# Scan states in SBUF, the C row in a PSUM bank, products with C on pairs of tiles

## The chip, the cores and the metric

One core of one Trainium2 chip runs the whole program. The metric is the device time of one execution in microseconds. The engines of the core work side by side and meet at semaphores: TensorE (PE) multiplies matrices, VectorE (DVE), ScalarE (ACT) and GpSimd (POOL) work on tiles, SyncE (SP) issues most DMAs.

## The reference

The input is x of 8 sequences of 512 positions and 512 features. Three parts are added to it one after the other:

```python
x = x + 0.5 * ffn(layernorm(x))          # G
x = x + attn(layernorm(x))               # M: a state-space layer
x = x + 0.5 * ffn(layernorm(x))          # F

# ffn: h = silu(x @ w_gate) * (x @ w_up); of each 4 neighbours the 2 of largest magnitude stay; h @ w_down
# attn:
skip = xn @ W_skip.T;  u = silu(causal_conv4(xn @ W_in.T) + conv_b)
delta = softplus(u @ Wd1.T @ Wd2.T + bd2);  Bt = u @ WB.T;  Ct = u @ WC.T;  A = -exp(A_log)
h[l] = exp(delta[l] * A) * h[l-1] + (delta[l] * u[l]) * B[l]     # 1024 channels x 16 states
y[l] = sum over the 16 states of h[l] * C[l]
out = ((y + u * W_D) * silu(skip)) @ W_out.T
```

All of it is fp32.

## The kernel before

Features lie on the 128 partitions and the 512 positions of a sequence on the free axis, so a tile is 128x512 f32 and fills one PSUM bank. The sequences b = 0 to 7 pass through three stages: G (first FFN), M (the state-space layer) and F (second FFN). `ORDER` lists the 16 FFNs. The program is a list of 575 ticks that class `Plan` writes out by hand-set numbers; every engine's block walks the same ticks and issues, in its own fixed order, what the tick holds. A tick holds one product (a gate or up tile of an FFN, 12 matmuls, L678 `product`), side jobs (`win`, `down`, `in`, `skip`, `dt`, `bc`, `dl`, `out` and the norms' sums), and some units of the scan. `PAUSES` puts ticks without a product between, `STARTS[b]` is the tick at which the scans of sequence b begin, and `VECTOR`, `TENSOR` and `READ` are the planner's costs: by them it deals the units out to the ticks and chooses side banks.

A **unit** is one scan of a 128x512 tile: one of 8 channel tiles with one of 16 states, so 128 units a sequence and 1024 in all, in two halves of 64 a sequence. Four neighbouring units (HE) share a state and thus one row of B and of C; `load_rows` (ACT's DMA queue) brings both rows, broadcast over the partitions, to `scan_rows`. A unit u goes through four engines:

- ScalarE, `unit` (L911): `decay[u % 3]`, a PSUM bank, gets exp(delta * A). It waits until the product with C of unit u - 3 has read the bank (L920). `upto` issues these up to two units ahead of the scans (EXP_LEAD).
- GpSimd, `scan_input` (L1450): `scan_in[u % 4]` = du * B, once scan u - 4 is done.
- VectorE, `scan` (L1330): the scan, in place in the PSUM bank `decay`.
- VectorE, `times_c` (L1336): `scan_out[u % 6]` = state * C row, 128x512, once GpSimd has freed that slot (L1342).
- GpSimd, `sum_states` (L1462): adds two slots at once to `y`, 128x1024. It is issued three pairs late (LAG).

VectorE's queue holds, in each tick, the units in four shares (`begin`, `finish`), and between them: `select` (L1276), `add_down` (L1311), `add_out` (L1320), `centre`, `compare` (L1264), `input_low` and `x_low` (zlo, xlo: what the rounded high parts leave), `multiply` (L1257), `gate`, `delta_times_u` and the taps of the convolution (L1359). In `begin` a share of two units runs scan, scan, product, product; a share of one unit runs scan, other work if the tick has any, product.

FFN products and projections are made of three matmuls for each of the 4 k: high weights with the high part of the input, high weights with its low part (`zlo`, `xlo`), low weights with the high part (L690 to L692, L795 to L797). The first product of an FFN waits for `zlo` tile by tile (L689). The wins of the 2-of-4 selection (L743) wait for all three comparisons, the first `down` of a stage (L772) for all four selections.

The convolution's output goes to `cv[e % 2]` and from there to DRAM (L553), `skip` through `skb` (L545, L1087). PSUM has eight banks: five for products and side jobs, three for `decay`.

Of the kernel before, what the change touches and what calls it, by code (L numbers as in the profile page):

```python
# [19 lines left out]
B, L, D = 8, 512, 512  # L20
E, N, DT, DC = 1024, 16, 128, 4
I = 2048
P = 128
KD = D // P
# [12 lines left out]
BANKS = 3  # L37
# [27 lines left out]
PAUSES = {0: 9, 34: 1, 45: 7, 224: 4, 384: 1, 416: 1, 448: 4, 480: 24}  # L65
# [13 lines left out]
STARTS = (67, 130, 191, 250, 312, 359, 409, 454, 515)  # L79
# [7 lines left out]
VECTOR = {"mean": 2.3, "down": 0.3, "out": 0.7, "win": 0.6, "in": 1.1, "up": 0.7, "step": 2.9, "low": 2.0, "scale": 3.0, "gate": 2.2, "du": 3.0, "unit": 1.99}  # L87
TENSOR = {"dt": 6.9, "bc": 1.8, "fold": 1.2, "msum": 0.9, "mean": 0.6, "vsum": 0.9, "var": 0.9, "dl": 0.0, "win": 0.7, "down": 3.5, "in": 3.5, "skip": 3.5,
          "out": 3.5, "product": 2.8}
READ = {"win": 0.2, "down": 0.25, "out": 0.25, "mean": 0.3, "msum": 0.1, "vsum": 0.1, "in": 0.9, "var": 1.9, "skip": 0.6, "dt": 0.6, "bc": 0.6, "fold": 0.6, "dl": 0.6,  # L90
        "gate": 0.35, "up": 1.35, "first up": 0.55}
# [212 lines left out]
def build(nc, x_in, ffn_w, down_w, mam_w, out_w, wdt_in, wbc_in, wd2_in, small_in, out):  # L304
# [6 lines left out]
    with ctx:  # L311
# [6 lines left out]
        def pb(name):  # L318
# [61 lines left out]
        decay = [pb(f"decay{k}") for k in range(BANKS)]  # L380

# [5 lines left out]
            "decay_ready", "input_ready", "state_ready", "weighted_ready", "sum_ready",  # L387
# [6 lines left out]
            "skip_stored", "u_stored_0", "u_stored_1", "u_loaded_0", "u_loaded_1", "u_loaded_2",  # L394
# [28 lines left out]
        def conv_of(b, e):  # L423

            return cv[e % 2][:] if b else du[:, e, :]
# [41 lines left out]
        def u_stores(b, e):  # L467

            return 4 * (b - 1) + e // 2 if b else 0
# [8 lines left out]
        def _(sp):  # L478
# [60 lines left out]
            for tick in range(plan.ticks):  # L539
                n = plan.product_at[tick]  # L540
                jobs = plan.jobs_at[tick - 1] if tick else []
                for key in plan.jobs_at[tick - 2] if tick > 1 else []:
                    if key[0] == "skip":
                        wait_read(sp, key)
                        sp.dma_start(skip_dram[key[1]][:, key[2], :], skb[:]).then_inc(sem["skip_stored"], 16)  # L545
# [3 lines left out]
                for key in plan.jobs_at[tick - 5] if tick > 4 else []:  # L549
                    if key[0] == "in" and key[1]:  # L550
                        b, e = key[1:]
                        sp.wait_ge(sem["u_ready"], KE * b + e + 1)
                        sp.dma_start(u_dram[b % 2][:, e, :], cv[e % 2][:]).then_inc(sem[f"u_stored_{e % 2}"], 16)  # L553
# [79 lines left out]
                for b in range(B):  # L633
# [12 lines left out]
                    if b + 1 < B and tick == max(plan.out_at[b, 0] + KD, plan.tick_of_job["in", b + 1, KE - 1] + 6):  # L646
                        for k in range(2):
                            sp.wait_ge(sem[f"u_stored_{k}"], 16 * 4 * (b + 1))
# [910 lines left out]
```

## Time and profile before

| | us |
|---|---|
| median of 3 runs | 3488.46 (3487.1 to 3489.23) |
| the profiled execution | 3488.33 |
| its span, first to last instruction | 3486.3 |
| granted TensorE clock, mean over the span | 0.988 |

| engine | busy us | share |
|---|---|---|
| TensorE | 3331.9 | 96% |
| VectorE | 2999.3 | 86% |
| GpSimd | 2584.7 | 74% |
| ScalarE | 1992.0 | 57% |

The times of single instructions are those of the profile. An instruction's duration runs to the acknowledgement of its writes, and the next one on the same engine may start before that, so durations of neighbours overlap; how far is seen from the starts in the timeline. A wait's releaser is the instruction whose semaphore came last.

### The profile page before, as it was taken

What the parts mean: (1) busy time and instruction counts of PE and PEld (TensorE: products, weight loads), DVE (VectorE), ACT (ScalarE), POOL (GpSimd) and SP (SyncE); (2) the same over time, 40 slices, a digit from 0 to 9 for tenths busy, and PEclk for the clock granted to TensorE, in tenths of its full rate; (3) what the DMA queues carried; (4) which work ended last, traced back from release to release, by engine and by line L of the source; (5) the groups of instructions that cost most, each with busy time, mean ns of one, the idle gap of its engine ahead of it and who ended that gap; (6) DMA issues with size and microseconds to landing.
All of it is one profiled execution on the core that took longest, in us unless ns stands there. A gap on an engine that the chain in (4) does not pass through costs nothing. (4 is left out here: it accounts for less than half of the span.)

```text
span 3486.3 us, 38913 instructions
## 1 busy us (share of the span) xinstructions
PE 3331.9 (96%) x11958; PEld 2112.4 (61%) x12020; DVE 2999.3 (86%) x3549; ACT 1992.0 (57%) x2755; POOL 2584.7 (74%) x1625
## 2 busy tenths in 40 slices
PE   8999999999999999999999998999989889989899
PEld 6775656557656665566656665556555555555467
DVE  4646998789889899989989999999999998999934
ACT  5545657557565574666555675566465575554422
POOL 1315786667887778778787898888889888989913
PEclk9999999999999999999999999999999999999999
DMA  9655566646756566467566675656646566655433
GB/s 362 223 194 190 167 218 212 230 170 219 234 179 230 177 228 233 151 221 224 199 212 204 198 242 178 212 172 222 225 140 220 175 215 212 181 159 191 135 122 117
DMA packets 243469, 696.44 MB, mean 200 GB/s; under 512 B 23536, under 2 KB 23792, under 8 KB 233584
## 3 DMA queue, kind: packets, MB, share of 16 engines
q1 hardware_dynamic: 173632, 559.72, 46.2%
q10 hardware_dynamic: 69632, 134.23, 14.4%
q8 instruction: 99, 1.62, 0.2%
q14 instruction: 106, 0.87, 0.1%
HBM read 619.94 MB, written 76.55 MB: 200 GB/s over the span
## 5 line engine op out<-in xcount | busy, mean ns | idle before, releaser
L1460 POOL TENSOR_TENSOR scan_in<-du,scan_rows 128x512 f32<-128x512 f32 x1024 | 1309.6, 1295 | 602.3 <-DVE decay L1333 506.5
L1333 DVE TENSOR_TENSOR_SCAN decay<-decay,scan_in 128x512 f32<-128x512 f32 x1024 | 1246.0, 1221 | 16.9 <-POOL scan_in L1460 8.7
L1473 POOL TENSOR_TENSOR y<-y,scan_out 128x1024 f32<-128x1024 f32 x512 | 1223.8, 2390 | 0.9 <-DVE scan_out L1343 0.9
L921 ACT ACTIVATE decay<-delta,small 128x512 f32<-128x512 f32 x1024 | 696.9, 688 | 866.8 <-DVE scan_out L1343 859.4
L690 PE MATMUL side<-zhi,wunit 128*128 128x512 f32 x2048 | 906.3, 443 | 36.5 <-DVE zlo L1237 12.8
L780 PE MATMUL side<-h,wdown 128*128 128x512 f32 x1760 | 800.4, 598 | 22.5 <-DVE res_r L1318 11.2
L692 PE MATMUL side<-zhi,wunit 128*128 128x512 f32 x2048 | 816.4, 399 | 0.0
L691 PE MATMUL side<-zlo,wunit 128*128 128x512 f32 x2048 | 815.3, 398 | 0.0
L1343 DVE TENSOR_TENSOR scan_out<-decay,scan_rows 128x512 f32<-128x512 f32 x1024 | 700.6, 685 | 36.3 <-POOL y L1473 14.2
L780 PEld LDWEIGHTS side<-h,wdown 128*128 128x128 f32 x1760 | 333.2, 191 | 392.5 <-issue 348.5
L908 ACT ACT_TABLE_LOAD x402 | 515.8, 1283 | 7.1
L690 PEld LDWEIGHTS side<-zhi,wunit 128*128 128x128 f32 x2048 | 388.8, 190 | 203.6 <-issue 81.6
L691 PEld LDWEIGHTS side<-zlo,wunit 128*128 128x128 f32 x2048 | 389.6, 190 | 126.4 <-issue 42.6
L692 PEld LDWEIGHTS side<-zhi,wunit 128*128 128x128 f32 x2048 | 389.1, 190 | 94.9
L1273 DVE TENSOR_TENSOR cmp<-ab,side 128x512 bf16<-128x512 f32 (+2 forms) x192 | 232.4, 1210 | 41.6 <-ACT side L968 41.4
L795 PE MATMUL side<-xhi,wmam 128*128 128x512 f32 x512 | 235.8, 461 | 18.4 <-DVE cv L1367 6.0
L808 PE MATMUL side<-y,wmam 128*128 128x512 f32 x512 | 232.9, 599 | 13.2 <-DVE y L1375 6.4
L1478 POOL TENSOR_TENSOR hlo<-h,hhi 128x512 fp32r<-128x512 f32 x32 | 45.3, 1442 | 253.3 <-ACT hhi L1020 253.2
L968 ACT ACTIVATE side<-h 128x512 f32<-128x512 f32 x192 | 113.1, 589 | 179.3 <-DVE h L1261 179.0
L751 PE MATMUL side<-cmp,signs 128*128 128x512 bf16 x670 | 173.8, 395 | 37.2 <-DVE cmp L1273 19.5
L797 PE MATMUL side<-xhi,wmam 128*128 128x512 f32 x512 | 204.8, 400 | 0.0
L796 PE MATMUL side<-xlo,wmam 128*128 128x512 f32 x512 | 203.9, 398 | 0.0
(109 smaller groups left out, 2828.3 us busy)
## 6 DMA issues: line engine op xcount, KB each, us to landing
wunit<-hl_dram SPq DMA_DIRECT2D x480, 512.0 KB, 4.1
scan_rows<-bc_dram ACTq DMA_DIRECT2D x256, 512.0 KB, 5.6
wdown<-down_w_dram SPq DMA_DIRECT2D x256, 256.0 KB, 3.0
wmam<-mam_dram SPq DMA_DIRECT2D x128, 512.0 KB, 4.2
hl_dram<-wunit SPq DMA_DIRECT2D x32, 512.0 KB, 5.9
skip_dram<-skb SPq DMA_DIRECT2D x64, 256.0 KB, 4.3
delta<-skip_dram SPq DMA_DIRECT2D x16, 1024.0 KB, 8.0
wmam<-wout_dram SPq DMA_DIRECT2D x32, 512.0 KB, 4.4
```

What stands on the lines that cost most here:

```text
L690: nc.tensor.matmul(main(n)[:], hi[:, k, :], zhi[:, k, :], start=(k == 0), stop=False)
L691: nc.tensor.matmul(main(n)[:], hi[:, k, :], zlo[:, k, :], start=False, stop=False)
L692: mm = nc.tensor.matmul(main(n)[:], lo[:, k, :], zhi[:, k, :], start=False, stop=(k == KD - 1))
L780: mm = nc.tensor.matmul(bank[:], wdown[t][:, j, :], h[s % 2][:, j, :], start=(j == 0), stop=(j == 3))
L795: nc.tensor.matmul(bank[:], w[:, k, :], xhi[:, k, :], start=(k == 0), stop=False)
L808: mm = nc.tensor.matmul(bank[:], w[:, odd * KD + t, :].bitcast(f32), y[:, e, :], start=(c + odd == 0), stop=(c + odd == 2))
L908: nc.scalar.preload_act_table_set(name)
L921: nc.scalar.activation(decay[u % BANKS][:], delta[:, e, :], ACT.Exp, scale=aneg[:, e * N + n:e * N + n + 1]).then_inc(sem["decay_ready"], 1)
L1333: nc.vector.tensor_tensor_scan(decay[u % BANKS][:], decay[u % BANKS][:], db[u % INPUTS][:], 0.0, ALU.mult, ALU.add).then_inc(sem["state_re ...
L1343: nc.vector.tensor_tensor(pr[u % RING][:], decay[u % BANKS][:], rows[m % ROWS][:, 1, :], ALU.mult).then_inc(sem["weighted_ready"], 1)
L1460: nc.gpsimd.tensor_tensor(db[u % INPUTS][:], du[:, e, :], rows[m % ROWS][:, 0, :], ALU.mult).then_inc(sem["input_ready"], 1)
L1473: nc.gpsimd.tensor_tensor(y[:, e:e + 2, :], y[:, e:e + 2, :], scan_out[:, k:k + 2, :], ALU.add).then_inc(sem["sum_ready"], 1)
```

## The change

- The scan writes its states to `scan_out[u % 6]` in SBUF and no longer over `decay`. So the even scan of a pair waits for the slot pair (`sum_ready`), and a `decay` bank is free after the scan. There are two `decay` banks instead of three.
- The freed bank, `decay_row`, holds the C row. ScalarE copies it from `scan_rows` once for four units (`copy_c_row`), after the last product with the row before, and ahead of the exponentials of the share.
- The product with C is made in place in `scan_out`, 128x1024, with the row broadcast over two tiles: 512 instead of 1024 instructions. Inside a share it comes after the next even scan, else at the share's end.
- A third buffer `cv` for the convolution takes the place of `skb`; `skip` rows pass through `zm` (first sequence) or `dts` (others), with waits for that.
- TensorE's order in products and projections: all high parts first, the matmuls with the low part of the input last; the first product of an FFN waits for the high parts, then for the low ones. The wins and the first `down` wait for their inputs one by one.
- Planner numbers: three pauses, three starts by one tick, costs and read times.

```diff
-BANKS = 3
+TAPS = 3
+BANKS = 2
+C_AFTER = 0
-PAUSES = {0: 9, 34: 1, 45: 7, 224: 4, 384: 1, 416: 1, 448: 4, 480: 24}
+PAUSES = {0: 9, 36: 1, 45: 7, 224: 4, 392: 1, 416: 1, 452: 4, 480: 24}
-STARTS = (67, 130, 191, 250, 312, 359, 409, 454, 515)
+STARTS = (67, 130, 191, 250, 311, 359, 408, 454, 516)
-VECTOR = {"mean": 2.3, "down": 0.3, "out": 0.7, "win": 0.6, "in": 1.1, "up": 0.7, "step": 2.9, "low": 2.0, "scale": 3.0, "gate": 2.2, "du": 3.0, "unit": 1.99}
+VECTOR = {"mean": 2.0, "down": 0.3, "out": 0.7, "win": 0.5, "in": 0.0, "up": 0.0, "step": 3.2, "low": 2.0, "scale": 3.3, "gate": 2.9, "du": 2.0,
+          "unit": 1.99}
...
-        cv = [sb(f"cv{k}", [P, L]) for k in range(2)]
-        skb = sb("skb", [P, L])
+        cv = [sb(f"cv{k}", [P, L]) for k in range(TAPS)]
+        skip_buffer = lambda b: dts[:] if b else zm[:, 0, :]
+        c_row = pb("decay_row")
...
                 for k in range(KD):
                     if n % FFN == 0:
+                        pe.wait_ge(sem["high_part_ready"], KD * i + k + 1)
+                    nc.tensor.matmul(main(n)[:], hi[:, k, :], zhi[:, k, :], start=(k == 0), stop=False)
+                    nc.tensor.matmul(main(n)[:], lo[:, k, :], zhi[:, k, :], start=False, stop=False)
+                for k in range(KD):
+                    if n % FFN == 0:
                         pe.wait_ge(sem["normed_ready"], KD * i + k + 1)
-                    nc.tensor.matmul(main(n)[:], hi[:, k, :], zhi[:, k, :], start=(k == 0), stop=False)
-                    nc.tensor.matmul(main(n)[:], hi[:, k, :], zlo[:, k, :], start=False, stop=False)
-                    mm = nc.tensor.matmul(main(n)[:], lo[:, k, :], zhi[:, k, :], start=False, stop=(k == KD - 1))
+                    mm = nc.tensor.matmul(main(n)[:], hi[:, k, :], zlo[:, k, :], start=False, stop=(k == KD - 1))
                 mm.then_inc(sem["product_ready"], 1)
...
-                if j == 0:
-                    pe.wait_ge(sem["compared"], 3 * s + 3)
+                    if j == 0:
+                        pe.wait_ge(sem["compared"], 3 * s + k + 1)
...
-                    act.wait_ge(sem["weighted_ready"], u - BANKS + 1)
+                    act.wait_ge(sem["state_ready"], u - BANKS + 1)
...
+            def copy_c_row(m):
+
+                act.wait_ge(sem[f"rows_loaded_{m % ROWS}"], 16 * (m // ROWS + 1))
+                if m:
+                    act.wait_ge(sem["weighted_ready"], HE * m)
+                nc.scalar.activation(c_row[:], rows[m % ROWS][:, 1, :], ACT.Copy).then_inc(sem["c_row_ready"], 1)
...
             def upto(end):
 
+                while HE * copied[0] + C_AFTER < end:
+                    copy_c_row(copied[0])
+                    copied[0] += 1
...
-                    act.wait_ge(sem[f"u_stored_{e % 2}"], 16 * u_stores(b, e))
+                    act.wait_ge(sem[f"u_stored_{e % TAPS}"], 16 * u_stores(b, e))
...
-                nc.scalar.activation(skb[:], bank_of(key)[:], ACT.Silu).then_inc(read_of(key), 1)
+                if e == 0:
+                    if b:
+                        wait_job(act, ("dl", b - 1, KE - 1))
+                    else:
+                        act.wait_ge(sem["x_low_ready"], KD)
+                nc.scalar.activation(skip_buffer(b), bank_of(key)[:], ACT.Silu).then_inc(read_of(key), 1)
...
+                if key[1]:
+                    act.wait_ge(sem["skip_stored"], 16 * KE * (key[1] + 1))
                 nc.scalar.activation(dts[:], bank_of(key)[:], ACT.Copy).then_inc(read_of(key), 1)
...
             def scan(u):
                 dve.wait_ge(sem["decay_ready"], u + 1)
                 dve.wait_ge(sem["input_ready"], u + 1)
-                nc.vector.tensor_tensor_scan(decay[u % BANKS][:], decay[u % BANKS][:], db[u % INPUTS][:], 0.0, ALU.mult,
+                if u >= RING and u % 2 == 0:
+                    dve.wait_ge(sem["sum_ready"], (u - RING) // 2 + 1)
+                nc.vector.tensor_tensor_scan(pr[u % RING][:], decay[u % BANKS][:], db[u % INPUTS][:], 0.0, ALU.mult,
                                              ALU.add).then_inc(sem["state_ready"], 1)
 
-            def times_c(u):
-                m = u // HE
-                if u % HE == 0:
-                    dve.wait_ge(sem[f"rows_loaded_{m % ROWS}"], 16 * (m // ROWS + 1))
-                dve.wait_ge(sem["state_ready"], u + 1)
-                if u >= RING:
-                    dve.wait_ge(sem["sum_ready"], (u - RING) // 2 + 1)
-                nc.vector.tensor_tensor(pr[u % RING][:], decay[u % BANKS][:], rows[m % ROWS][:, 1, :], ALU.mult).then_inc(sem["weighted_ready"], 1)
+            def times_c(p):
+                u = 2 * p
+                k = u % RING
+                dve.wait_ge(sem["c_row_ready"], u // HE + 1)
+                dve.wait_ge(sem["state_ready"], u + 2)
+                nc.vector.tensor_tensor(scan_out[:, k:k + 2, :], scan_out[:, k:k + 2, :], c_row[:].unsqueeze(1).broadcast_to([P, 2, L]),
+                                        ALU.mult).then_inc(sem["weighted_ready"], 2)
 
             def begin(units):
 
                 for u in units:
-                    second = (u - units.start) % 2
-                    if u > units.start and not second:
-                        times_c(u - 1)
                     scan(u)
-                    if second:
-                        times_c(u - 1)
+                    if u % 2 == 0 and u > units.start:
+                        times_c(u // 2 - 1)
 
             def finish(units):
-                if units:
-                    times_c(units[-1])
+                if units and units[-1] % 2:
+                    times_c(units[-1] // 2)
```

## Rows read from the trace of the kernel before

**Rows 1.** The page's first part: busy us, share of the span, instructions.

```profile
PE 3331.9 (96%) x11958; PEld 2112.4 (61%) x12020; DVE 2999.3 (86%) x3549; ACT 1992.0 (57%) x2755; POOL 2584.7 (74%) x1625
```

**Rows 2.** By stretch: length, busy us (count) of each engine, clock, DMA share, GB/s.

```profile
300.00:2080.00 1780.00, 1751.48 (x6298) 1103.05 (x6331) 1618.53 (x1910) 1097.11 (x1480) 1402.94 (x867) 1.00 0.63 207
...
2080.00:3280.00 1200.00, 1106.97 (x3777) 673.57 (x3797) 1142.73 (x1324) 694.55 (x953) 1057.74 (x655) 0.97 0.60 193
3280.00:3486.00 206.00, 186.94 (x708) 128.89 (x708) 96.00 (x136) 56.73 (x96) 64.17 (x44) 0.98 0.34 110
```

**Rows 3.** Timeline of VectorE: start us, us, line, operation, out<-in, how many merged.

```profile
2612.56 1.22 DVE L1333 TENSOR_TENSOR_SCAN decay<-decay,scan_in 128x512 f32<-128x512 f32 x1
2613.82 0.69 DVE L1343 TENSOR_TENSOR scan_out<-decay,scan_rows 128x512 f32<-128x512 f32 x1
2614.42 1.22 DVE L1333 TENSOR_TENSOR_SCAN decay<-decay,scan_in 128x512 f32<-128x512 f32 x1
...
2916.28 2.34 DVE L1333 TENSOR_TENSOR_SCAN decay<-decay,scan_in 128x512 f32<-128x512 f32 x2
```

**Rows 4.** Groups by line and form: busy us, mean ns | idle before, releasers.

```profile
L1333 DVE TENSOR_TENSOR_SCAN decay<-decay,scan_in 128x512 f32<-128x512 f32 x1024 | 1246.0, 1221 | 16.9 <-POOL scan_in L1460 8.7 <-ACT decay L921 8.0
...
L1343 DVE TENSOR_TENSOR scan_out<-decay,scan_rows 128x512 f32<-128x512 f32 x1024 | 700.6, 685 | 36.3 <-POOL y L1473 14.2
...
L908 ACT ACT_TABLE_LOAD x402 | 515.8, 1283 | 7.1
...
L968 ACT ACTIVATE side<-h 128x512 f32<-128x512 f32 x192 | 113.1, 589 | 179.3 <-DVE h L1261 179.0
...
L1273 DVE TENSOR_TENSOR cmp<-ab,side 128x1024 bf16<-128x1024 f32 x64 | 77.4, 1210 | 12.8 <-ACT side L968 12.8
...
L1231 DVE TENSOR_TENSOR zm<-zm,side 128x2048 f32<-128x2048 f32 x14 | 31.9, 2278 | 0.0
...
L1228 DVE TENSOR_TENSOR zm<-zm,side 128x512 f32<-128x512 f32 x8 | 5.0, 682 | 11.0 <-ACT side L1062 11.0
...
L1309 DVE TENSOR_TENSOR hlo<-h,hhi 128x512 fp32r<-128x512 f32 x4 | 2.7, 688 | 0.3 <-ACT hhi L1020 0.3
```

**Rows 5.** Waits between 2080 and 3280 us: who waited for whom, us, times, longest.

```profile
DVE scan_out L1343 <- POOL y L1473: 10.9, 13, 1.7
```

**Rows 6.** Timelines of VectorE and GpSimd: scans against the sums that free their slots.

```profile
2923.14 1.22 DVE L1333 TENSOR_TENSOR_SCAN decay<-decay,scan_in 128x512 f32<-128x512 f32 x1
2924.27 0.67 DVE L1318 SCALAR_TENSOR_TENSOR res_r<-side,res_r 128x512 f32<-128x512 f32 x1
2926.68 0.69 DVE L1343 TENSOR_TENSOR scan_out<-decay,scan_rows 128x512 f32<-128x512 f32 x1 [1.73 <-POOL y L1473]
...
2924.20 2.38 POOL L1473 TENSOR_TENSOR y<-y,scan_out 128x1024 f32<-128x1024 f32 x1
...
1918.90 1.22 DVE L1333 TENSOR_TENSOR_SCAN decay<-decay,scan_in 128x512 f32<-128x512 f32 x1
...
1916.64 2.37 POOL L1473 TENSOR_TENSOR y<-y,scan_out 128x1024 f32<-128x1024 f32 x1
...
3283.53 1.22 DVE L1333 TENSOR_TENSOR_SCAN decay<-decay,scan_in 128x512 f32<-128x512 f32 x1
...
3282.56 2.34 POOL L1473 TENSOR_TENSOR y<-y,scan_out 128x1024 f32<-128x1024 f32 x1
```

**Rows 7.** Waits over the whole span, longest in total first.

```profile
ACT decay L921 <- DVE scan_out L1343: 859.4, 544, 6.3
...
ACT cv L1073 <- DMA u_dram<-cv: 15.6, 8, 3.8
...
PE side L690 <- DVE zlo L1237: 12.8, 5, 6.7
...
DVE decay L1333 <- ACT decay L921: 8.0, 8, 1.9
...
PE side L795 <- DVE cv L1367: 6.0, 2, 3.9
```

More of the change, by code:

```diff
@@ L85 @@
 SPLIT_AT = 10
-VECTOR = {"mean": 2.3, "down": 0.3, "out": 0.7, "win": 0.6, "in": 1.1, "up": 0.7, "step": 2.9, "low": 2.0, "scale": 3.0, "gate": 2.2, "du": 3.0, "unit": 1.99}
[L88 to L91, printed above, removed]
+VECTOR = {"mean": 2.0, "down": 0.3, "out": 0.7, "win": 0.5, "in": 0.0, "up": 0.0, "step": 3.2, "low": 2.0, "scale": 3.3, "gate": 2.9, "du": 2.0,
+          "unit": 1.99}
+TENSOR = {"dt": 7.6, "bc": 1.2, "fold": 1.2, "msum": 0.9, "mean": 0.6, "vsum": 0.9, "var": 0.9, "dl": 0.0, "win": 0.7, "down": 3.5, "in": 3.2,
+          "skip": 3.6, "out": 3.9, "product": 2.8}
+READ = {"win": 0.1, "down": 0.2, "out": 0.25, "mean": 0.9, "msum": 0.2, "vsum": 0.5, "in": 0.9, "var": 1.9, "skip": 0.5, "dt": 0.3, "bc": 0.8,
+          "fold": 0.3, "dl": 0.6, "gate": 0.15, "up": 1.35, "first up": 0.75}
 EXP_TABLE, SILU_TABLE, SOFTPLUS_TABLE = "natural_log_exp_and_others", "silu_and_others", "softplus"
@@ L423, in conv_of @@
         def conv_of(b, e):
[L425 removed]
+            return cv[e % TAPS][:] if b else du[:, e, :]
         def last_down(i):
@@ L646, in _ @@
                     if b + 1 < B and tick == max(plan.out_at[b, 0] + KD, plan.tick_of_job["in", b + 1, KE - 1] + 6):
-                        for k in range(2):
-                            sp.wait_ge(sem[f"u_stored_{k}"], 16 * 4 * (b + 1))
+                        for k in range(TAPS):
+                            sp.wait_ge(sem[f"u_stored_{k}"], 16 * len(range(k, KE, TAPS)) * (b + 1))
                         sp.wait_ge(sem["input_ready"], UNITS * b + HALF)
@@ L793, in project @@
                     if kind == "in" and e == 0:
+                        pe.wait_ge(sem["x_high_ready"], KD * b + k + 1)
+                    nc.tensor.matmul(bank[:], w[:, k, :], xhi[:, k, :], start=(k == 0), stop=False)
+                    nc.tensor.matmul(bank[:], w[:, KD + k, :], xhi[:, k, :], start=False, stop=False)
+                for k in range(KD):
+                    if kind == "in" and e == 0:
                         pe.wait_ge(sem["x_low_ready"], KD * b + k + 1)
-                    nc.tensor.matmul(bank[:], w[:, k, :], xhi[:, k, :], start=(k == 0), stop=False)
-                    nc.tensor.matmul(bank[:], w[:, k, :], xlo[:, k, :], start=False, stop=False)
-                    mm = nc.tensor.matmul(bank[:], w[:, KD + k, :], xhi[:, k, :], start=False, stop=(k == KD - 1))
+                    mm = nc.tensor.matmul(bank[:], w[:, k, :], xlo[:, k, :], start=False, stop=(k == KD - 1))
                 mm.then_inc(sem["side_ready"], 1)
```

24 lines of the change are left out of this document (13 added, 11 removed).

## The prediction, made before the changed kernel ran

> **What bounds the kernel now.** I read the page's first part first. TensorE is busy 96% of the span, VectorE 86%, GpSimd 74%, ScalarE 57%: no engine has much to give, and the shares are means over stages [rows 1]. So next the busy time by stretches [rows 2]. From 300 to 2080 us TensorE is busy 1751 of 1780 us at a full clock; VectorE, at 1619, has 161 us to spare. That stretch is TensorE's, and a cheaper VectorE buys there at most the 28 us in which TensorE stands. From 2080 to 3280 us it is the other way round: VectorE is busy 1143 of 1200 us (57 idle), TensorE 1107 at a granted clock of 0.97 (93 idle), GpSimd 1058. Each sequence of 128 scans has fewer products beside it there, so VectorE sets the pace and TensorE waits for its results. The last 206 us hold the tail, with few scans. The change must therefore be costed on VectorE's queue between 2080 and 3280 us. GpSimd ran 655 instructions there, two inputs and one sum for each pair of units, so some 437 units or 218 pairs.
>
> Third, what a VectorE instruction costs. The listed durations overlap: three neighbours in [rows 3] start 1.26 us (scan, then its own product with C) and 0.60 us (product, then next scan) apart, and two merged scans take 2.34 us, so 2.34 - 1.22 = 1.12 us is one scan's real share and 0.60 that of a product with C. A scan that is directly followed by a product that needs its own result costs 1.26 and not 1.12: the product waits out the scan's end, 0.13 us more. Over the run 477 of the 1024 scans are followed so (counted in the timeline; [rows 3] shows one).
>
> **The change part by part.**
>
> *Products with C, 1024 of 128x512 become 512 of 128x1024.* The nearest forms are the 128x1024 comparison, 1210 ns, and the scaling of `zm`, 682 ns for 128x512 and 2278 ns for 128x2048 (an SBUF tensor in place, with a PSUM operand broadcast over it: the new form), which gives 1.04 ns an element and 1214 ns for 1024 [rows 4]. The duration falls by 2 x 685 - 1214 = 156 ns a pair, and a reader of busy shares would book 80 us for the run. But 0.09 us of each duration is overlap with the next instruction, so the queue gains 2 x 0.595 - 1.125 = 0.065 us a pair: 218 x 0.065 = 14 us in the VectorE stretch, 33 in the run. Bounds: 12 to 34 (all the duration).
>
> *Fewer direct waits.* At most one product a pair can now stand right behind its own scan. At the old share of 477/1024, 102 of 218 pairs pay 0.13 us where 204 of 437 units did: 102 x 0.13 = 13 us saved in the stretch. The shares into which a tick's units are cut are mostly one unit long, so it may be that every pair closes right behind its second scan: then 218 against 204, a loss of 2 us. Bounds -2 to +20, taken 12.
>
> *The scan writes SBUF.* Its inputs stay (one PSUM, one SBUF). An all-SBUF subtraction with nothing beside it took 688 ns, the products with one PSUM input 685, the scaling 682 [rows 4], so the place changes a fixed cost by 6 ns at most: nothing, bounds -3 to +3 us in the stretch. The Trainium skill ("Perfetto Trace Analysis", Optimizing Scalar/DVE Operations) puts VectorE's access overhead at about 60 ns on SBUF and 125 on PSUM; by that the 437 scans would gain up to another 28 us. The rows here show no such difference, so the sum goes by the rows.
>
> *The ring wait moves.* Before, a product with C waited for a slot of `scan_out`; now the even scan does, two to three instructions earlier, and behind it queue the scan, the product of the pair in front, and whatever selection, sum or residual TensorE waits for. The old ring already runs full: products wait 10.9 us for GpSimd's sums in this stretch [rows 5], and [rows 6] shows the worst case: scan at 2923.14, the sum that frees its slot only from 2924.20 to 2926.58. Now scan and residual add (2924.27) go behind that sum, 3.4 us later, of which 1.7 was idle before anyway. I compared all 256 even scans of the second half with the end of the sum which they will wait for: 67 start ahead of it; first (1918.90 against 1919.01), last (3283.53 against 3284.90) and worst are in [rows 6]. They come in bursts, and a delay is paid once a burst: 15 bursts between 2080 and 3280, of 1.6 us on average, 24 us; less the 10.9 already paid, 13 us. Below: nothing, if the freed 26 us let VectorE meet GpSimd later (it makes it meet earlier, so this is unlikely); above: each of the 67 pays for itself, 72 - 11 = 61 us. GpSimd is never idle in these bursts, so its 1058 us stay.
>
> *C rows by ScalarE.* 256 copies SBUF to PSUM, as the 589 ns form [rows 4]: 110 x 0.59 = 65 us of the 505 us in which ScalarE is idle in the stretch (1200 - 695, [rows 2]), hidden there. On the path is only its latency: with one bank, a copy starts after the second product of the old row and must end before the first of the new one, two scans, 2.25 us, later. ScalarE often sits in a table load plus two SiLU plus a load back at that time, about 1.3 + 1.2 + 1.3 us by the table load's 1283 ns and the 0.59 us form [rows 4]. VectorE waits 8.0 us over 8 times for `decay` in the whole run [rows 7], with a lead of two scans and two products, 3.4 us; for the copy it is 1.2 us less, once in four units. Taken 6 us; bounds 0 to 18 (a third of 110 copies by 0.5). Two `decay` banks for three cost nothing by themselves: a bank now comes free at the scan's end, and between that and the scan that needs the new one lie a scan and a product, 2.2 us for a 0.69 us exponential. ScalarE's 859 us of waiting for the old products [rows 7] shows its reserve.
>
> *TensorE's order.* The first product of each of the 16 FFNs and of each projection needs only the high parts for 8 of its 12 matmuls; 12.8 us of TensorE idle end at `zlo`, in 5 places [rows 7], and go only as far as 8 matmuls last, since the last four still want `zlo`. Taken 5 us, under half; bounds 0 to 13. The waits for comparisons and selections one by one go with it: 1 us.
>
> *Third convolution buffer.* The first tap waits 15.6 us for stores of `cv`; TensorE stands 6.0 us at L795 until a bank is freed by the taps [rows 7]. The store has then a job more of time: the waits go, taken 4, bounds 0 to 9. The skip rows go through `zm` and `dts`, idle then; if that cover is gone, the copy to `dts` waits for the last store.
>
> *Planner numbers.* They shift a unit or so from tick to tick; the starts move by one tick in three of nine. Taken 0, bounds -8 to +8.
>
> Sum in the VectorE stretch: -14 - 12 + 13 + 6 - 5 - 1 - 4 = -17; TensorE standing less also drops fewer stretches to its 1.2 GHz level (0.97 against 1.00 [rows 2]): -2. Elsewhere TensorE bounds, and VectorE's 20 us go into its idle time: -1. Together **-20 us** on the profiled 3488.33 (span 3486.3 and 2.0 around it), which is the median of the runs, 3488.46, within 0.2: **3468 us**.
>
> **The rivals.**
>
> A, *the ring ends the gain* (slower). Mechanism: `sum_states` of pair p stands behind two more inputs in GpSimd's queue, and VectorE stalls at the even scan whenever it runs ahead. If bursts don't absorb each other, 61 us and 10 for C rows against 39 gained elsewhere: +32, 3520. It decides from about 33 us of net stall at the ring. For it: 67 late of 256, GpSimd 88% busy. Against: one delay a burst. Half-way, at 45 us of stall, 3500.
>
> B, *nothing moves* (within 0.2%): every pair closes right behind its scan (+14 against my sum) and the TensorE parts give 3 instead of 10: 3489. For it: shares of one unit.
>
> C, *VectorE's relief frees TensorE wholly*: ring stall 0, C rows 0, TensorE parts at their bounds: -14 - 12 - 13 - 9 - 8 = -56, 3432. For it: 93 us of TensorE idle in the stretch, all behind VectorE. Against: GpSimd's 1058 of 1200.
>
> D, *a scan into SBUF is cheaper*. From rows: 512 elements at two steps of 1.04 ns are 1.065 of a scan's 1.12 us; were the other 0.055 to go, 0.055 x 437 = 24: 3444. Against: the 688 ns row. It is what the rule of the Trainium skill ("Perfetto Trace Analysis", Optimizing Scalar/DVE Operations) would do here.
>
> **How the numbers follow.** Forecast (gain 8 to 40) 0.45, C 0.14, D 0.04, B 0.16, A 0.21. A measurement of this kernel tells 0.2%, 7 us, from no change. Faster 0.63, same 0.16, slower 0.21. The range takes in C's near edge and the milder A: 3434 to 3502.
>
> **What would show it.** Right: product with C at about 1214 ns x512, scans at 1221; VectorE's busy time down by 80 us though the span falls by 20; a new wait of the scan line for `y` of GpSimd, 15 to 35 us in all; the product with C waiting for the C row under 15 us; idle at `zlo` under 8; copies 0.59 us each. Wrong: scan-line waits of more than 50 us, or the C product over 1.25 us, or scans whose duration has moved, or GpSimd's inputs above 1.30 us because scans now write SBUF beside it.

## The result: 0.7% slower, and the profile after

The changed kernel takes 3512.16 us (median of 5, 3508.45 to 3516.21) against 3488.46: ratio 1.0067, 95% interval 1.0054 to 1.0080. The forecast was 3468 with a range up to 3502. The profiled execution has a span of 3507.8 us.

Two stretches of the kernel after, with the columns of [rows 2]:

```profile
300.00:2080.00 1780.00, 1744.56 (x6269) 1093.75 (x6268) 1568.37 (x1607) 1166.43 (x1610) 1389.07 (x859) 1.00 0.64 205
2080.00:3280.00 1200.00, 1111.29 (x3807) 669.65 (x3806) 1113.71 (x1102) 756.41 (x1063) 1053.76 (x651) 0.98 0.60 193
```

VectorE's work fell: 1568 us where it was 1619, and 1114 where it was 1143 [rows 2]; over the span it is 2940 us for 2999, 60 less where the forecast's sign had 80. But in the 1200 us which it was to bound, the 29 us that it is less busy are 29 us more of idle time. Nothing used them: GpSimd, whose 1024 inputs and 512 sums are unchanged, did 1054 us of work there and 1058 before, so the scans moved no faster. In the first stretch too TensorE did 1745 instead of 1751 us in the same time.

The groups of the kernel after, which answer to [rows 4] (busy us, mean ns | idle before, releasers):

```profile
L1365 DVE TENSOR_TENSOR_SCAN scan_out<-decay,scan_in 128x512 f32<-128x512 f32 x1024 | 1222.1, 1211 | 63.8 <-ACT decay L930 41.9 <-POOL y L1501 21.2
...
L1373 DVE TENSOR_TENSOR scan_out<-scan_out,decay_row 128x1024 f32<-128x1024 f32 x512 | 622.1, 1215 | 39.8 <-ACT decay_row L940 7.5 <-DVE scan_out L1365 1.0
...
L940 ACT ACTIVATE decay_row<-scan_rows 128x512 f32<-128x512 f32 x256 | 152.7, 596 | 162.2 <-DVE scan_out L1373 159.3 <-DMA scan_rows<-bc_dram 2.7
```

The product with C is what the forecast made of it: 1215 ns for 1214, 512 of them. The scan into SBUF is listed at 1211 ns instead of 1221. The new number is on the right: VectorE stood 17 us in front of its scans before and stands 64 now, 42 of them for exponentials. The waits of the kernel after over the whole span, which answer to [rows 7]:

```profile
ACT decay L930 <- DVE scan_out L1365: 764.4, 619, 7.5
...
ACT decay_row L940 <- DVE scan_out L1373: 159.3, 131, 5.3
...
DVE scan_out L1365 <- ACT decay L930: 41.9, 39, 6.9
...
DVE scan_out L1365 <- POOL y L1501: 21.2, 28, 2.5
...
PE side L786 <- ACT h L978: 15.9, 7, 5.2
...
DVE scan_out L1373 <- ACT decay_row L940: 7.5, 5, 2.6
...
PE side L694 <- ACT h L978: 6.9, 4, 3.4
...
PE side L699 <- DVE zlo L1267: 0.9, 2, 0.5
```

Four things stand there. Scans wait for exponentials 41.9 us over 39 times, against 8.0 over 8 [rows 7]. They wait for GpSimd's sums 21.2 us; the products did so for 14.2 [rows 4]. The wait for the C row is small, 7.5. And TensorE waits for `h`, ScalarE's SiLU of a gate tile, 22.8 us at these two lines and 28.5 us at all of them, which the kernel before never did. Not all of that belongs to the scan part, as the experiments show.

One of the longest of these SiLU waits shows how work of ScalarE comes late. The timelines of ScalarE, VectorE and TensorE of the kernel after (start us, us, line, operation, out<-in, how many merged, idle before):

```profile
2477.10 0.69 ACT L930 ACTIVATE decay<-delta,small 128x512 f32<-128x512 f32 x1 [7.52 <-DVE scan_out L1365]
...
2478.21 0.69 ACT L930 ACTIVATE decay<-delta,small 128x512 f32<-128x512 f32 x1 [0.42 <-DVE scan_out L1365]
2481.06 0.69 ACT L930 ACTIVATE decay<-delta,small 128x512 f32<-128x512 f32 x1 [2.15 <-DVE scan_out L1365]
2482.17 0.69 ACT L930 ACTIVATE decay<-delta,small 128x512 f32<-128x512 f32 x1 [0.42 <-DVE scan_out L1365]
2483.58 0.60 ACT L940 ACTIVATE decay_row<-scan_rows 128x512 f32<-128x512 f32 x1 [0.72 <-DVE scan_out L1373]
2484.66 0.69 ACT L930 ACTIVATE decay<-delta,small 128x512 f32<-128x512 f32 x1 [0.47 <-DVE scan_out L1365]
...
2485.37 1.28 ACT L917 ACT_TABLE_LOAD   x1
2486.66 1.08 ACT L978 ACTIVATE h<-side 128x512 f32<-128x512 f32 x2
...
2473.64 2.29 DVE L1403 TENSOR_TENSOR y<-y,delta 128x2048 f32<-128x2048 f32 x1 [5.74 <-DMA delta<-skip_dram]
2475.85 2.33 DVE L1365 TENSOR_TENSOR_SCAN scan_out<-decay,scan_in 128x512 f32<-128x512 f32 x2
...
2479.81 2.33 DVE L1365 TENSOR_TENSOR_SCAN scan_out<-decay,scan_in 128x512 f32<-128x512 f32 x2
2482.27 1.22 DVE L1373 TENSOR_TENSOR scan_out<-scan_out,decay_row 128x1024 f32<-128x1024 f32 x1
2483.41 2.33 DVE L1365 TENSOR_TENSOR_SCAN scan_out<-decay,scan_in 128x512 f32<-128x512 f32 x2
...
2467.20 1.10 PE L699 MATMUL side<-zlo,wunit 128*128 128x512 f32 x4
...
2470.65 1.10 PE L699 MATMUL side<-zlo,wunit 128*128 128x512 f32 x4
...
2481.45 1.10 PE L699 MATMUL side<-zlo,wunit 128*128 128x512 f32 x4
2487.80 2.07 PE L786 MATMUL side<-h,wdown 128*128 128x512 f32 x2 [5.25 <-ACT h L978]
```

Products run gate, gate, up, up. The two gate tiles end with the matmuls of 2467.20 and 2470.65, the first up tile with those of 2481.45. The two SiLUs stand in ScalarE's queue behind six more instructions, which all belong to the scans; each exponential starts as a scan ends, 0.42 to 7.5 us after ScalarE was free for it. The first long wait isn't ScalarE's own: VectorE had stood 5.74 us for a DMA (2473.64) before it reached its scans. The last exponential, 2484.66, needs the bank of the scan that began at 2483.41. Only then come the table load and, at 2486.66, the two SiLUs, 18.4 and 15.4 us after their products. TensorE, done with the up tile at 2482.55, stood for 5.25 us until the bank of a gate tile was free for the `down` at 2487.80.

The same place exists with three banks: in e2, described below, TensorE stands 2.99 us there (VectorE waits 6.56 us for the same DMA), in e13 5.10. So about 2 of these 5.25 us come with the two-bank rule, and the rest is there without it. A measure over all 256 SiLUs says more: the median time from the end of a gate product to its SiLU is 3.8 us in the kernel before and 4.8 after. ScalarE has idle time enough (it is busy 61% of the span), but it spends it waiting for scans, while TensorE's tile lies behind. That is one way in which lateness shows, not the whole loss; how far it can carry the 40 us found below is weighed in the section on why.

### The profile page after: what moved, and what is told of

Read it like the earlier page. It is cut to its first block, busy times and chain, and to the rows that moved or that the text cites. A ratio compares the mean times of both kernels' runs of the same rounds, so it can differ in the third digit from the quotient of the medians.

```text
span 3507.8 us, 38373 instructions
## 1 busy us (share of the span) xinstructions
PE 3347.4 (95%) x12020; PEld 2110.1 (60%) x12020; DVE 2939.8 (84%) x3037; ACT 2135.8 (61%) x3013; POOL 2588.2 (74%) x1625
## 4 chain that ended last, share of the span: by engine, by line
PE 49%; DVE 17%; POOL 14%; issue 12%; ACT 6%; DMA 2%; DVEq 0%; SPq 0%; ACTq 0%; POOLq 0%
PE side L786 10%; POOL scan_in L1488 9%; DVE scan_out L1365 8%; PE side L694 7%; PE side L699 7%; PE side L695 7%; POOL y L1501 5%; PE side L817 4%; DVE scan_out L1373 2%; ACT L917 2%; PE side L758 2%; PE side L801 2%; PE side L806 2%; PE side L802 2%; DVE cmp L1303 2%
## 5 line engine op out<-in xcount | busy, mean ns | idle before, releaser
L1488 POOL TENSOR_TENSOR scan_in<-du,scan_rows 128x512 f32<-128x512 f32 x1024 | 1310.8, 1297 | 618.3 <-DVE scan_out L1365 522.6
L1365 DVE TENSOR_TENSOR_SCAN scan_out<-decay,scan_in 128x512 f32<-128x512 f32 x1024 | 1222.1, 1211 | 63.8 <-ACT decay L930 41.9
L694 PE MATMUL side<-zhi,wunit 128*128 128x512 f32 x2048 | 906.6, 443 | 26.2 <-ACT h L978 6.9
L786 PE MATMUL side<-h,wdown 128*128 128x512 f32 x1760 | 808.5, 604 | 30.9 <-ACT h L978 15.9
L1373 DVE TENSOR_TENSOR scan_out<-scan_out,decay_row 128x1024 f32<-128x1024 f32 x512 | 622.1, 1215 | 39.8 <-ACT decay_row L940 7.5
L699 PE MATMUL side<-zlo,wunit 128*128 128x512 f32 x2048 | 565.5, 397 | 1.8 <-DVE zlo L1267 0.9
L694 PEld LDWEIGHTS side<-zhi,wunit 128*128 128x128 f32 x2048 | 388.1, 190 | 190.4 <-issue 61.2
L940 ACT ACTIVATE decay_row<-scan_rows 128x512 f32<-128x512 f32 x256 | 152.7, 596 | 162.2 <-DVE scan_out L1373 159.3
L758 PE MATMUL side<-cmp,signs 128*128 128x512 bf16 x732 | 184.2, 386 | 25.8 <-DVE cmp L1303 13.4
```

The source lines that it names most:

```text
L694: nc.tensor.matmul(main(n)[:], hi[:, k, :], zhi[:, k, :], start=(k == 0), stop=False)
L699: mm = nc.tensor.matmul(main(n)[:], hi[:, k, :], zlo[:, k, :], start=False, stop=(k == KD - 1))
L786: mm = nc.tensor.matmul(bank[:], wdown[t][:, j, :], h[s % 2][:, j, :], start=(j == 0), stop=(j == 3))
L1365: nc.vector.tensor_tensor_scan(pr[u % RING][:], decay[u % BANKS][:], db[u % INPUTS][:], 0.0, ALU.mult, ALU.add).then_inc(sem["state_ready" ...
L1373: nc.vector.tensor_tensor(scan_out[:, k:k + 2, :], scan_out[:, k:k + 2, :], c_row[:].unsqueeze(1).broadcast_to([P, 2, L]), ALU.mult).then_ ...
L1488: nc.gpsimd.tensor_tensor(db[u % INPUTS][:], du[:, e, :], rows[m % ROWS][:, 0, :], ALU.mult).then_inc(sem["input_ready"], 1)
```

## The experiments

Each run is timed beside the kernel before on the same chip, 4 to 11 executions; ratios are to that, and times of runs on different chips are compared by them. The first theory, Q, says that ScalarE's queue is held by the scans (two banks and the C row copies; Q2 is the half with the two banks), R that the ring wait is the cost, P that it lies outside the scan part.

### e1 and e2: which half of the change

e1 is the kernel before with the scan part alone (states in SBUF, two banks, copied C rows, pair products):

```diff
-BANKS = 3
+BANKS = 2
+C_AFTER = 0
...
+        c_row = pb("decay_row")
...
-                    act.wait_ge(sem["weighted_ready"], u - BANKS + 1)
+                    act.wait_ge(sem["state_ready"], u - BANKS + 1)
```

and with `copy_c_row`, `upto`, `scan`, `times_c`, `begin` and `finish` of the changed kernel.

> The kernel before with only the scan part of the change: states to SBUF, two decay banks, C rows copied by ScalarE, products 128x1024. Old planner numbers, old order of TensorE, old convolution and skip buffers. Theory Q (ScalarE's queue: two banks and the copies at the head of a share hold ScalarE until the scans of that share have run, so SiLUs and exponentials come late): 3510 to 3530, with TensorE waiting 15 us or more for the SiLU and scans waiting over 25 us for exponentials. Theory R (the ring wait alone): also 3510 or more, but then scan waits for GpSimd's sums over 30 us and no new waits for ScalarE. Theory P (planner numbers or the other edits cost the time): at most 3475.

Measured: 3534.06 us, ratio 1.0126 (1.0113 to 1.0140).

e2 is the opposite: the changed kernel with these pieces taken back.

```diff
-BANKS = 2
-C_AFTER = 0
+BANKS = 3
...
-        c_row = pb("decay_row")
```

> The changed kernel with the scan part taken back: three decay banks, products 128x512 with C from SBUF rows; new TensorE order, third convolution buffer and new planner numbers stay. Theories Q and R: faster than before, 3470 to 3485 (the 10 us that the prediction gave to TensorE's order and the buffer). Theory P: 3500 or more.

Measured: **3472.92 us**, ratio 0.9951 (0.9937 to 0.9964). It is faster than the kernel before and by 39 us than the changed one. P falls: the scan part alone costs 44 us on the old kernel and about 40 on the new rest. e1 is 4 us above Q's 3510 to 3530. Its scans waited 60.0 us for exponentials, as Q had it, but TensorE waited 1.2 us for the SiLU and not 15 or more. For sums the scans waited 25.8 us where R wanted over 30, and R's "no new waits for ScalarE" was wrong. Neither was right in full, and R wasn't out yet.

### e3 and e8: the copies of the C row

e3 copies the row only once:

```diff
                 while HE * copied[0] + C_AFTER < end:
-                    copy_c_row(copied[0])
+                    if not copied[0]:
+                        copy_c_row(0)
...
-                dve.wait_ge(sem["c_row_ready"], u // HE + 1)
+                dve.wait_ge(sem["c_row_ready"], 1)
```

> The changed kernel, but the C row is copied to its bank only once, at the start; all products use that row, so the output is not the reference's. This leaves out 255 copies of 0.6 us and ScalarE's 159 us of waiting in front of them. Theory Q, if the copies are the larger part of it: 3480 to 3495. If the two banks are the larger part, 3503 to 3510. Theory R: 3508 to 3512, since the ring is untouched.

Measured: 3509.38 us, ratio 1.0055 (1.0043 to 1.0068), 3 us less than the changed kernel (1.0054 to 1.0080); the intervals overlap, so it is little or nothing. The time is also one that R allowed. The 159 us that ScalarE waited in front of the copies only moved: the waits for scans in front of exponentials grew by 283 us, and TensorE's for the SiLU stayed. Three lines of e3's waits, to be held against the ones above:

```profile
ACT decay L930 <- DVE scan_out L1366: 1047.5, 641, 8.1
...
DVE scan_out L1366 <- ACT decay L930: 39.2, 34, 6.9
...
PE side L786 <- ACT h L979: 16.9, 7, 5.2
```

e8 puts the copy behind the share's own exponentials:

```diff
+                for u in range(units_done[0], max(units_done[0], end)):
+                    unit(u)
+                    units_done[0] = u + 1
                 while HE * copied[0] + C_AFTER < end:
```

> The changed kernel with the C row copied behind the exponentials of the share's own units and ahead of the two of lead. Since copying once took 3 us off, both theories expect little: 3506 to 3514.

Measured: 3510.37 us, ratio 1.0060 (1.0046 to 1.0074). The copies as such are 3 us of the loss or less, and their place is nothing that can be told.

### e4: the C row from SBUF

No copies and three decay banks; the pair product reads the row from `scan_rows`, whose reload now waits for the products:

```diff
-                dve.wait_ge(sem["c_row_ready"], u // HE + 1)
+                m = u // HE
+                if u % HE == 0:
+                    dve.wait_ge(sem[f"rows_loaded_{m % ROWS}"], 16 * (m // ROWS + 1))
...
-                nc.vector.tensor_tensor(scan_out[:, k:k + 2, :], scan_out[:, k:k + 2, :], c_row[:].unsqueeze(1).broadcast_to([P, 2, L]),
+                nc.vector.tensor_tensor(scan_out[:, k:k + 2, :], scan_out[:, k:k + 2, :], rows[m % ROWS][:, 1, :].unsqueeze(1).broadcast_to([P, 2, L]),
...
+                if m >= ROWS:
+                    act.wait_ge(sem["weighted_ready"], HE * (m - ROWS + 1))
                 act.dma_start(rows[m % ROWS][:]
```

> The changed kernel with the product reading the C row from scan_rows in SBUF, no copies, and the freed bank given back to decay (three banks). Costs 512 products with two SBUF inputs beside GpSimd: by the 2830 against 2278 ns of the 128x2048 forms up to 0.28 us each, 60 us of VectorE in the stretch that it bounds. Theory Q: ScalarE's lateness is gone (TensorE waits for SiLU under 3 us, scans wait for exponentials under 12 us) whatever the time; time 3490 to 3540 by the port. Theory R: scan waits for sums as in the changed kernel or more.

Measured: 3795.81 us, ratio 1.0879 (1.0865 to 1.0894). The second SBUF input costs far more than the 0.28 us a product that was expected, and the time is far above the expected 3490 to 3540. The groups of e4:

```profile
L1481 POOL TENSOR_TENSOR scan_in<-du,scan_rows 128x512 f32<-128x512 f32 x1024 | 1645.2, 1623 | 431.4 <-DVE scan_out L1356 340.1 <-DMA scan_rows<-bc_dram 76.7 <-DVE du L1402 13.7
L1494 POOL TENSOR_TENSOR y<-y,scan_out 128x1024 f32<-128x1024 f32 x512 | 1359.1, 2655 | 1.2 <-DVE scan_out L1366 1.2
...
L1366 DVE TENSOR_TENSOR scan_out<-scan_out,scan_rows 128x1024 f32<-128x1024 f32 x512 | 1068.1, 2086 | 29.4 <-DVE scan_out L1356 1.0
...
L1356 DVE TENSOR_TENSOR_SCAN scan_out<-decay,scan_in 128x512 f32<-128x512 f32 x1024 | 1216.6, 1206 | 30.2 <-POOL y L1494 21.6 <-POOL scan_in L1481 5.8 <-ACT decay L929 2.7
```

The product takes 2086 ns where it took 1215, and GpSimd's input 1623 where it took 1297 in the changed kernel: both engines pay, 446 us of VectorE and 334 of GpSimd's inputs over the run. That is what the bank for the C row buys. On Q the run speaks through its last line: with three decay banks scans wait 2.7 us for exponentials. TensorE still waits 15.8 us for the SiLU at its `down` line, 25.9 in all, where under 3 were expected, so that wait isn't the banks' alone. But it isn't a clean test of either: VectorE is slowed so much that exponentials have more time, and the new wait in front of the reload of `scan_rows` stands in ScalarE's queue: 166 us of ScalarE's idle time, 71 times, end at a product there.

### e5, e6 and e9: a third decay bank, with one side bank less

PSUM is full, so a bank had to be taken from the side jobs first. e5 is the changed kernel with `POOL = 4`, e6 that with `BANKS = 3`.

```diff
-POOL = 5
+POOL = 4
```

> Base for the next one: the changed kernel with four side banks of PSUM instead of five, two decay banks and one C row bank. TensorE waits more for free side banks: any theory 3515 to 3600.

Measured: 3694.66 us, ratio 1.0592 (1.0577 to 1.0606), 95 us above the expected range.

```diff
-BANKS = 2
+BANKS = 3
```

> As the run before it, with the fourth bank given to decay: three decay banks. Only the number of decay banks differs between the two. Theory Q2 (two decay banks cost the time: ScalarE is tied to the scan of its own share): at least 20 us faster than the one before it, and scans wait under 15 us for exponentials (41.9 in the changed kernel). Theory R (ring wait at the scan): within 6 us of it, scans' waits for GpSimd's sums stay at 20 us or more.

Measured: 3628.72 us, ratio 1.0400 (1.0386 to 1.0415): 66 us faster than e5. The waits of e5 and then those of e6 in two fences:

```profile
ACT decay L930 <- DVE scan_out L1365: 815.5, 615, 9.4
...
DVE scan_out L1365 <- ACT decay L930: 48.2, 41, 8.6
...
PE side L694 <- ACT h L978: 30.2, 17, 5.3
...
DVE scan_out L1365 <- POOL y L1501: 14.3, 19, 2.2
```

```profile
ACT decay_row L940 <- DVE scan_out L1373: 409.2, 162, 8.4
...
ACT decay L930 <- DVE scan_out L1365: 285.1, 201, 8.4
...
DVE scan_out L1365 <- ACT decay L930: 26.7, 21, 8.3
...
DVE scan_out L1365 <- POOL y L1501: 20.9, 27, 2.4
...
PE side L694 <- ACT h L978: 17.8, 10, 4.7
```

ScalarE's wait in front of exponentials falls from 815 to 285 us, but its wait in front of the C row copies rises from 177 to 409, so the two together fall from 993 to 694. Scans wait 27 instead of 48 us for exponentials and TensorE 18 instead of 30 for the SiLU at L694 (25 instead of 47 at all lines). Waits for the sums (R) rise from 14 to 21 us while the kernel becomes faster. The scans' wait is above the 15 us that was expected.

e9 gives the other side of the same size: four side banks, three decay banks, and the old scan part (e2 with `POOL = 4`).

> The counterpart of the run with four side and three decay banks (3628.7): all of the change but the scan part (products 128x512 with C from SBUF rows, states in PSUM), with four side and three decay banks; its eighth bank stays unused. If the scan part itself is a gain once three decay banks stay (VectorE's 33 us and the direct waits), this is slower than 3629, 3640 or more. If the ring wait, the later products or the copies cost as much as they save, 3620 to 3635. If the scan part is a loss besides the bank, under 3615.

Measured: 3638.25 us, ratio 1.0425 (1.0410 to 1.0439). It lies between what was expected of a gain (3640 or more) and of a draw (up to 3635). With equal banks the new scan part is about 9 us faster than the old by the ratios (1.0400 against 1.0425, whose intervals just touch), with its ring wait, its copies and its later products all in it. So at three banks it is at best a small gain, and no loss. Either is less than a side bank is worth: e9 is 165 us above e2, which has one more.

### e7: the ring

```diff
-LAG = 3
+LAG = 2
```

> The changed kernel with LAG 2 instead of 3: GpSimd adds a pair's products one pair earlier in its queue, so a slot pair of scan_out comes free about 2.5 us earlier against its inputs. Theory R: 15 us or more faster than the changed kernel (at most 3497), scans' waits for sums near zero. Theory Q2: within 6 us of 3512, or slower, as GpSimd now waits for products.

Measured: 3512.99 us, ratio 1.0073 (1.0060 to 1.0085). No scan waits for a sum any more; GpSimd has taken the waiting over, in front of its sums. The waits of e7:

```profile
POOL scan_in L1488 <- DVE scan_out L1365: 348.8, 147, 9.7
...
POOL y L1501 <- DVE scan_out L1373: 176.7, 147, 6.0
...
DVE scan_out L1365 <- ACT decay L930: 43.8, 41, 7.0
...
PE side L786 <- ACT h L978: 18.4, 8, 5.2
```

349 + 177 = 526 us, where the changed kernel has 523 in front of the inputs alone: GpSimd idles as before in sum. The exponentials and the SiLU are as late as in the changed kernel, and so is the end. R falls.

### e10: less lead

With two banks, an exponential one unit ahead of the share doesn't hold ScalarE until the share's scan has run.

```diff
-EXP_LEAD = 2
+EXP_LEAD = 1
```

(on e8).

> The changed kernel with exponentials issued one unit ahead of the share instead of two, the C row copied behind the share's own exponentials. With two banks and a lead of two, ScalarE stays in a share until the scan of that share has run; with a lead of one it leaves at once, but each next scan finds one exponential ready and not two. If ScalarE's being held (late SiLU) is what costs: 3480 to 3500. If the missing exponential costs: 3525 or more, and scans wait over 60 us for exponentials.

Measured: 3545.90 us, ratio 1.0159 (1.0145 to 1.0173). Scans wait 172.7 us over 175 times for exponentials. TensorE's waits for the SiLU fall from 31 us in e8 to 14, so ScalarE is freed; but letting it go earlier loses more than it gains: what two banks lack is depth, and no order of ScalarE's queue tried here replaces it.

### e13: the rule alone

e6 against e5 was measured in a kernel that is slower by over 100 us. So the rule which two banks bring was put into e2, which has three banks, states in PSUM and products 128x512:

```diff
                 if u >= BANKS:
                     act.wait_ge(sem["weighted_ready"], u - BANKS + 1)
+                if u >= 2:
+                    act.wait_ge(sem["state_ready"], u - 1)
```

> All of the change but the scan part (3472.9), with one wait added: the exponential of unit u waits, besides its bank, until scan u - 2 has finished, as in the changed kernel, though three banks are there. Five side banks, scan in PSUM, products 128x512 as before. Theory Q2 (the rule that two decay banks bring is the cost): 3500 to 3525, scans wait over 25 us for exponentials. If the cost came from the scan part's other sides (ring, pair products, copies): at most 3480.

Measured: 3512.96 us, ratio 1.0066 (1.0052 to 1.0079), **40 us more than e2** and as much as the changed kernel. The waits of e2 and then those of e13:

```profile
ACT decay L928 <- DVE scan_out L1359: 878.3, 575, 10.0
...
PE side L784 <- ACT h L964: 10.8, 5, 3.1
...
DVE decay L1349 <- ACT decay L928: 5.1, 6, 1.9
```

```profile
ACT decay L930 <- DVE decay L1351: 1048.1, 641, 7.7
...
PE side L784 <- ACT h L966: 15.9, 8, 5.1
...
DVE decay L1351 <- ACT decay L930: 19.9, 34, 3.1
...
PE side L692 <- ACT h L966: 8.5, 4, 3.8
```

ScalarE's wait in front of exponentials goes from products to scans and is 22% longer with what is left of the old one (1048 + 27 against 878 us). That rest also says that e13 is a little stricter than the changed kernel, which doesn't wait for products here: 28 of its waits still end at a product, the longest after 1.3 us. Scans wait 19.9 us for exponentials, not over 25 as expected; the 34 places are nearly the changed kernel's 39. A direct measure says the same: in 13 of 1024 units of e2 (15 before) the exponential ends less than 0.2 us ahead of its scan; in e13 it is 52, in the changed kernel 53, in e1 59 and in e10 209. The median lead is 3.87 us before and in e2, 2.78 in e13 and 2.75 after. The median SiLU starts 3.6 us after its product in e2, 4.8 in e13 and 4.8 in the changed kernel.

### e11, e12 and e14: the rest

TensorE's order alone in the kernel before (L678, L743, L772 and L788 as in the change), the planner's numbers alone, and the third convolution buffer alone.

> The kernel before with only TensorE's new order (matmuls with the low part of the input last, first product waiting for the high parts, wins and first down waiting one by one). The prediction gave it 6 us: 3480 to 3486. If it carries the whole of the 15 to 17 us that all but the scan part gains: 3470 to 3476.

Measured: 3491.49 us, ratio 1.0003 (0.9994 to 1.0012): no gain, where 3480 to 3486 was expected.

> The kernel before with only the new planner numbers (pauses, starts, costs, read times). The prediction gave them nothing (3480 to 3496). Numbers fitted to another scan part may cost here: 3495 to 3515. If they carry the gain: 3470 to 3478.

Measured: 3482.54 us, ratio 0.9976 (0.9966 to 0.9985).

> The kernel before with only the third convolution buffer and the skip rows through zm and dts. What is left of the 17 us of all but the scan part after TensorE's order (nothing) and planner numbers (7): 3478 to 3484. The prediction gave it 4: 3484. If the parts only gain together: 3487 to 3490.

Measured: 3485.97 us, ratio 0.9990 (0.9981 to 0.9999).

In e11 TensorE's wait for `zlo` is this:

```profile
PE side L695 <- DVE zlo L1242: 2.4, 2, 1.9
```

2.4 us for 12.8 [rows 7]: the order did what it was to do, and the time didn't move. All waits of TensorE together are 140 us for 147; where the rest went isn't shown. The three parts add to -0.03 + 0.24 + 0.10 = 0.31%, and together they gave 0.49. Each of these four numbers is uncertain by about 0.1, so the difference isn't clear of noise, and no run tests whether the parts help each other.

## Why the prediction was wrong

- **The step that failed** is one sentence of the part on C rows: that two decay banks for three "cost nothing by themselves". It asked only whether a 0.69 us exponential fits into the 2.2 us (a scan and a product) between the release of its bank and its own scan. That leaves out two things. ScalarE may be elsewhere when the bank comes free, and the same paragraph puts such an absence at 1.3 + 1.2 + 1.3 us, more than 2.2; it counted this for the C row and not for the exponentials. And ScalarE works in order, so what stands behind a waiting exponential waits too. How long it waits follows from the shares, which are mostly one unit long, as the prediction says under "Fewer direct waits". In the share of a unit u, ScalarE issues the exponential of u + 2. With three banks it waits for the product of u - 1, which is over before the share begins; with two it waits for scan u, in the share itself and behind whatever VectorE does in between. Price by e13: 40 us, where 0 was entered.
- **By which way the 40 us come** is seen in the traces only in part. From e2 to e13 VectorE's waits for ScalarE in all grow from 104 to 125 us and TensorE's from 29 to 64: 57 us of new waits for 40 us of time. So both engines are served later, TensorE more. TensorE's waits for `h` are 17 us in e2 and 32 in e13; the 17 came with the planner numbers, not with the scan part (e12, which is faster than the kernel before, has 18), and e1, which loses 44 us, has 1.2. There it is VectorE that waits, 205 us against 127 before. The rule is the cause; where its lateness lands depends on the plan, and no run here divides the 40 us.
- ScalarE's 859 us of waiting for products [rows 7] was read as reserve. It was the measure of how closely ScalarE's queue hangs on VectorE's: an engine that waits in order for another has idle time, but not at the moment at which its next customer needs it. In e13 its part in front of exponentials grew by 22%, and the time by 40 us.
- **The merged products**: right in size (1215 ns) and in the warning not to book 80 us. The scan part with equal banks gained about 9 us (e6 against e9), and the sum's own items for it, -14 - 12 + 13 + 6, make -7; that these agree is partly luck, as three of the four were off.
- **Direct waits**: the count was right, the size off. 240 of 512 pair products stand right behind their second scan (239 by the forecast's share). But the timeline above has them 1.34 us behind the scan's start (2479.81 + 2.33 - 1.21 = 2480.93, product at 2482.27) and not 1.26, so each costs 0.21 us and not 0.13. In the run 477 x 0.13 - 240 x 0.21 = 12 us are saved, not 30; of the 12 us entered for the stretch about 5 are left.
- **The ring**: the wait came in the forecast size, 21.2 us within "15 to 35", but e7 removes it and nothing changes. 13 us were entered, and the rival A took it for the danger. The kernel did become slower, as A had it, and the sign "scan-line waits of more than 50 us" came true with 63.8 us. But 42 of these are for exponentials, which neither the forecast nor A had: A was near the time by luck.
- **C rows**: 6 us entered, 3 or less measured (e3), the product's wait 7.5 us.
- **The scan writes SBUF**: 0 entered, and none seen in its spacing. The 688 ns row it leaned on wasn't quite alone: ScalarE worked beside all four of its instructions, and GpSimd began at the end of two.
- **TensorE's order**: 6 us entered, 0 measured (e11). The idle time was real and 10 us of it went, but the time didn't follow. That another engine set the pace there is likely and not shown.
- **Third buffer**: 4 entered, 3 measured, 0 to 7 by its interval. **Planner numbers**: 0 entered, 7.5 gained (e12 against the kernel before on its chip), at the edge of the bounds of 8.
- Sum with what was measured: the rest -17, the scan part at three banks -9 to 0, the two-bank rule +40: +14 to +23, measured +24 (0.67% of 3488). If the small gain at three banks is real, it is lost again at two, or the terms don't simply add; no run tells which.

The loss isn't confined to where VectorE bounds. In the 1780 us up to 2080, TensorE did 6 us less than before. The two runs that differ by the rule alone show it better: scan 512 begins at 1886.2 us in e2 and at 1900.8 in e13, scan 576 at 2071.0 and 2092.0, the last one at 3286.3 and 3332.2. So e13 is 15, 21 and 46 us behind (its profiled execution is the slowest of its five), and nearly half of the loss has come by 2080. The prediction had written that stretch off as TensorE's own and costed the change on VectorE's queue after 2080 alone.

The faster version is e2: all of the change but the scan part, 3472.92 us, 0.49% below the kernel before and 1.1% below the changed one.

## What to carry to other kernels

Count a buffer's depth in the order in which the queues really run it, for the shortest share that the plan makes, and ask what else stands in the queue of the engine that waits for the buffer: the price of a missing bank shows on the engines that this queue serves, and little on the line that waits. An in-order engine's idle time in front of one kind of work is a sign of a tight bond, not of reserve. And before a stall is entered as a loss or its removal as a gain, ask whether the engine sets the pace there: the ring wait and the wait for `zlo` were both real, and taking either away moved nothing that could be measured.

## What the hardware showed that was not expected

A product 128x1024 with both operands in SBUF took 2086 ns beside GpSimd's work where the same with one in PSUM took 1215, and GpSimd's own 128x512 products went from 1297 to 1623 ns. The nearest rows before had let 0.28 us a product be expected, from 2830 ns for 128x2048 with both inputs in SBUF, shown here, against 2278 with one in PSUM [rows 4]; it was 0.87.

```profile
L1381 DVE TENSOR_TENSOR du<-delta,du 128x2048 f32<-128x2048 f32 x16 | 45.3, 2830 | 7.6 <-ACT y L1123 7.5
```

The Trainium skill ("SBUF — State Buffer", section Who interferes with whom) says that a VectorE instruction with two SBUF inputs contends with a GpSimd instruction that reads SBUF, and that issue order decides who blocks. Both engines' longer times in e4 agree with the first; no run here shows who blocked whom.

A product (128x1024) that waits for a scan's result in SBUF starts 1.34 us after that scan, one (128x512) that waits for a result in PSUM 1.26 us, though the scan itself is listed 10 ns shorter into SBUF. The scan's spacing to other work stayed at 1.13 us, so rival D's 0.055 us a scan didn't come.

The Trainium skill ("Perfetto Trace Analysis", section Optimizing Scalar/DVE Operations) has a lower overhead for VectorE on SBUF than on PSUM. Moving the scan's output gave nothing of it here; its decay input stayed in PSUM, so the rule isn't tested for an instruction all in SBUF.
